# A ring of 24 gathered rows in place of four buffers of six, in a two-layer graph attention kernel

## The chip, the cores and the metric

The kernel runs on one core of one Trainium2 chip. The metric is device time in microseconds. Three runs of the kernel before took 1912.78, 1916.56 and 1921.1 us, so their median is 1916.56 us. The profiled execution took 1914.35 us, of which 1912.5 us is the span from its first to its last instruction.

## The reference

Two graph attention layers over 8192 nodes with 256 features. The adjacency is an 8192x8192 matrix that is nearly empty: an edge is drawn with chance 0.000488281, then made symmetric, with ones on the diagonal.

```
# layer 0
h  = relu(layernorm(x));  Wh = h @ W
e  = (Wh @ a[:256])[:, None] + (Wh @ a[256:])[None, :]
x  = x + leaky_relu(softmax(where(adj == 0, -1e9, e)) @ Wh, 0.2)
# layer 1
h  = relu(layernorm(x))
e  = leaky_relu(h @ a[:256] + (h @ a[256:]).T, 0.01)
x  = x + softmax(where(adj > 0, e, -9e15)) @ h
```

## The kernel before

Rows are held 128 to a tile, 64 tiles in all. Layer 0 runs on TensorE over the whole adjacency (the first 1070 us or so of the span) and is not touched by the change. While it runs, the kernel also packs the adjacency into bits and makes, for the last 44 tiles of rows, a list of each row's neighbours, sorted by their number.

Layer 1 divides the rows. The first 20 tiles are done densely on TensorE: 5 groups of 4 tiles, each group 16 chunks, each chunk 64 pairs of a weight load and a matmul of 257 columns (line 1639). The other 44 tiles are done sparsely, beside it. For each sparse tile m there are `slots[m]` neighbours to a row (24 for the first tile, then 16, 14, 14, 13, 13, 12, ... 4; 420 in all), and for each of these 420 slots, called rows here and numbered 0 to 419:

- GpSimd issues one indirect DMA that gathers 128 rows of `h_d`, one to a partition, into the tile `gat` (line 1264).
- ScalarE makes two exponentials for a batch of gathered rows (line 1321, `weights`), once the batch has landed.
- VectorE takes their larger (line 1515, `larger`), then multiplies and adds the row into `sacc` (lines 1531 and 1534, `add_row`), which raises `row_added`. When a tile has all its rows, VectorE joins, divides and adds x (`join`, `divide`, `add_x1`, the last at the fifth row of the next tile), which raises `so_ready`, and GpSimd scatters the result to `out` (line 1255, `scatter`), `OUT_LAG` = 5 batches behind.

A batch is up to 6 rows of one tile; there are 88. The tile `gat` is four buffers of six rows. GpSimd waits before the first gather of batch k until the whole of batch k-4 has been added (lines 1261 and 1262).

The dense work of a chunk is written into the same instruction streams. ScalarE makes the signs of the next chunk (line 1300, four instructions), which wait for `unit_used`, raised by TensorE every half chunk; in group 0 it also makes the high halves of V (line 1289, eight). VectorE unpacks mask bits every second chunk (lines 1456 and 1459), makes the two masks (lines 1473 and 1478), in group 0 the low halves of V (line 1438, eight), and between these adds the rows that the table `rows_by` gives to the chunk: none in chunks 0 to 2, 5 in chunk 3, about 7 in each further chunk of group 0, and 5 or 6 in each later chunk. ScalarE runs ahead of VectorE by `LEAD` = 3 rows: a chunk's batches, through the one that holds the third row after the chunk, are weighed before the next chunk's signs. Nothing is reordered by a scheduler: each engine runs its own stream in the order of the code, and each waits at its head.

Of the kernel before, what the change touches and what calls it, by code (L numbers as in the profile page):

```python
# [30 lines left out]
def two_layer_graph_attention(nc, x, adj, w0, a0, a1, key_pos, ident, tri, caps, row_ids, out):  # L31
# [30 lines left out]
    P = 128  # L62
# [71 lines left out]
    with outer:  # L134
# [13 lines left out]
        with ctx:  # L148
            def sb(name, shape, dt):
                return ctx.enter_context(nc.sbuf_tensor(name, shape, dt))  # L150
# [881 lines left out]
        RB = 4  # L1032
        BIG = 2.0 ** 100
        BS = 6
        NBUF = 4
        LEAD = 3
        FIRST = 1.35
        HEAD = 3.0
# [5 lines left out]
        for m in range(NS):  # L1044
            parts = -(-slots[m] // BS)
            for i in range(parts):
                batch.append((m, slots[m] * i // parts, slots[m] * (i + 1) // parts))
        row = [(m, s, k) for k, (m, s0, s1) in enumerate(batch) for s in range(s0, s1)]
        begin = [row.index((m, s0, k)) for k, (m, s0, s1) in enumerate(batch)]
        at = [sum(slots[:m]) for m in range(NS + 1)]  # L1050
# [5 lines left out]

        def lead_of(q):

            return sum(1 for b in begin if b < q + LEAD) if q < len(row) else len(batch)

        def ended(q):

# [9 lines left out]
        with ctx:  # L1072
# [24 lines left out]
            sS = early[:, 9 * T:9 * T + 2 * NS].rearrange("p (s t) -> p s t", s=2)  # L1097
            tS = early[:, 11 * T:11 * T + NS]
            exc = early[:, 12 * T:12 * T + NS]
            gat = sb("gat", [P, NBUF, BS, ROW], f32)  # L1100
            sacc = sb("sacc", [P, 2, 2, DV], f32)
            sout = sb("sout", [P, NOUT, D], f32)
            e8 = sb("e8", [P, 2, 2, BS], f32)
# [47 lines left out]
            masks_seen = sem("masks_seen")  # L1151
            pos_taken = sem("pos_taken")
            evn_ready = sem("evn_ready")
            den2_ready = sem("den2_ready")
            den_ready = sem("den_ready")
            rd_ready = sem("rd_ready")
            fac_ready = sem("fac_ready")
            o_ready = sem("o_ready")
            o_out = sem("o_out")
# [88 lines left out]
            @block.gpsimd  # L1248
            def _(pool):
                pool.wait_ge(mx_ready, 1)  # L1250
                nc.gpsimd.partition_all_reduce(red[:, :], red_in[:, :], P, RMAX).then_inc(M_all, 1)

                def scatter(m):
                    pool.wait_ge(so_ready, m + 1)
                    pool.indirect_dma_start(  # L1255
                        out, bass.IndirectOffsetOnAxis(ap=rec[:, m, OWN:OWN + 1], axis=0),
                        sout[:, m % NOUT, :], None).then_inc(so_out[m % NOUT], 16)

                done = 0
                for k, (m, s0, s1) in enumerate(batch):  # L1260
                    if k >= NBUF:
                        pool.wait_ge(row_added, begin[k - NBUF + 1])
                    for s in range(s0, s1):
                        pool.indirect_dma_start(  # L1264
                            gat[:, k % NBUF, s - s0, :], None, h_d,
                            bass.IndirectOffsetOnAxis(ap=rec[:, m, s:s + 1], axis=0))\
                            .then_inc(gat_in[k % NBUF], 16)
                    while done < NS and last[done] + OUT_LAG <= k:
                        scatter(done)
                        done += 1  # L1270
                for m in range(done, NS):
                    scatter(m)

            @block.scalar
            def _(act):
# [37 lines left out]
                def weights(k):  # L1313


                    m, s0, s1 = batch[k]
                    act.wait_ge(gat_in[k % NBUF], 16 * fills[k])
                    if k >= 2:
                        act.wait_ge(w8_ready, k - 1)
                    for i, scale in ((0, 1.0), (1, SLOPE1)):  # L1320
                        nc.scalar.activation(e8[:, k % 2, i, 0:s1 - s0], gat[:, k % NBUF, 0:s1 - s0, DV],  # L1321
                                             ACT.Exp, scale=scale, bias=hb[:, i, m:m + 1]).then_inc(e8_ready, 1)

                def load_rows(m):
# [59 lines left out]
            def _(dve):  # L1384
# [95 lines left out]
                def take_sums(g):  # L1480
                    dve.wait_ge(unit_used, (g * NC + NC) * 2)
                    nc.vector.tensor_tensor(den2[:, :, :], ab[:, :, bass.ds(g * G, G)],
                                            banks[:, :, D].rearrange("p (g s) -> p s g", s=2), ALU.mult)\
                        .then_inc(den2_ready, 1)
                    dve.wait_ge(den2_ready, g + 1)
                    nc.vector.tensor_tensor(den[:, :], den2[:, 0, :], den2[:, 1, :], ALU.add)\
                        .then_inc(den_ready, 1)
                    dve.wait_ge(den_ready, g + 1)
                    nc.vector.reciprocal(rd[:, :], den[:, :]).then_inc(rd_ready, 1)
                    dve.wait_ge(rd_ready, g + 1)  # L1490
                    for s in range(2):
                        nc.vector.tensor_tensor(fac[:, s, :], ab[:, s, bass.ds(g * G, G)], rd[:, :],
                                                ALU.mult).then_inc(fac_ready, 1)
# [24 lines left out]
                def add_row(q):  # L1518


                    m, s, k = row[q]
                    i = s - batch[k][1]
                    acc = sacc[:, m % 2, s % 2, :]
                    if i == 0:
                        dve.wait_ge(w8_ready, k + 1)
                    x = gat[:, k % NBUF, i, 0:DV]
                    w = w8[:, k % 2, i:i + 1]
                    if s < 2:
                        if m >= 2 and s == 0:
                            dve.wait_ge(so_ready, m - 1)  # L1530
                        nc.vector.tensor_scalar(acc, x, w, None, ALU.mult).then_inc(row_added, 1)  # L1531
                    else:
                        dve.wait_ge(row_added, q - 1)
                        nc.vector.scalar_tensor_tensor(acc, x, w, acc, ALU.mult, ALU.add)\  # L1534
                            .then_inc(row_added, 1)
# [150 lines left out]
```

## Time and profile before

| | |
|---|---|
| median of 3 runs | 1916.56 us |
| profiled execution: its time, its span | 1914.35 us, 1912.5 us |
| TensorE, VectorE, ScalarE, GpSimd busy | 88%, 63%, 51%, 34% of the span |
| L1639, the dense matmuls of layer 1 | 5120 |
| L1264, the gathers | 420, 1109 ns each in the mean |
| L1255, the scatters | 44, 1058 ns each in the mean |
| chain that ended last | PE 28%, issue 8%, POOL 4%, DVE 2% of the span |

PE is TensorE, DVE VectorE, ACT ScalarE and POOL GpSimd. A busy share is of the whole span, and layer 1 is its last 45%. "Issue" is time in which an engine waited for nothing that the profile shows. "Remote" names a releaser that the profile could not find. The ends of matmuls are modelled, so TensorE's progress is better read from the number of matmuls in a stretch than from its busy time.

### The profile page before, as it was taken

To read this page: it belongs to the slowest core of one execution; us is meant where nothing else is said; L and a number is where in the kernel's file an instruction comes from. 1 tells how busy PE (TensorE), PEld (TensorE's weight loads), DVE (VectorE), ACT (ScalarE), POOL (GpSimd) and SP (SyncE) were. 2 spreads that over 40 slices of the span, in tenths; PEclk is the share of its full clock that TensorE was granted. 3 is DMA by queue.
4 is the path that set the end of the run, shared out by engine and by line. 5 is a ranking of instruction groups with operands and counts; after the bars stand their busy time and mean duration, and the time that the engine had idled before them with its cause. 6 is when DMAs were issued, how large, how long until landed. Compare 5 with 4: busy or idle time off the path is not lost. (4 is left out here: it accounts for less than half of the span.)

```text
span 1912.5 us, 37724 instructions
## 1 busy us (share of the span) xinstructions
PE 1691.5 (88%) x13955; PEld 1391.3 (73%) x13955; DVE 1203.0 (63%) x4595; ACT 973.4 (51%) x1367; POOL 651.6 (34%) x607
## 2 busy tenths in 40 slices
PE   6888999999999999999999397677888888978878
PEld 5646888888888888888888285454666667757657
DVE  7488888988888888674444377652435445435434
ACT  5987665665666556666662375432333233323322
POOL 0000000000000000026665548755656657665562
PEclk9998999999999999999999698877889889979889
DMA  8529998888988889989994534533333333433331
GB/s 287 182 76 386 342 349 325 314 311 321 354 320 326 318 310 331 355 333 378 386 379 104 130 94 134 160 80 88 101 89 83 111 89 94 117 100 99 88 92 52
DMA packets 142801, 410.60 MB, mean 215 GB/s; under 512 B 26193, under 2 KB 90066, under 8 KB 109906
## 3 DMA queue, kind: packets, MB, share of 16 engines
q1 hardware_dynamic: 108434, 329.85, 47.6%
q0 software_dynamic: 27904, 73.43, 13.9%
q10 hardware_dynamic: 6336, 5.77, 1.0%
q8 instruction: 62, 1.02, 0.2%
q14 instruction: 65, 0.53, 0.1%
HBM read 368.94 MB, written 40.03 MB: 214 GB/s over the span
## 5 line engine op out<-in xcount | busy, mean ns | idle before, releaser
L984 PE MATMUL banks<-HV,adjT 128*128 128x257 f16 x8192 | 938.8, 274 | 16.7 <-DVE adjT L658 8.8
L984 PEld LDWEIGHTS banks<-HV,adjT 128*128 128x128 fp8e4 x8192 | 792.5, 98 | 148.2 <-DVE HV L688 23.7
L1639 PE MATMUL banks<-Vp,adjp 128*128 128x257 f16 x2560 | 540.6, 292 | 115.4 <-issue 59.2
L1639 PE MATMUL banks<-Vn,adjn 128*128 128x257 f16 x2560 | 538.1, 291 | 48.9 <-issue 47.7
L1264 POOL DMA_INDIRECT gat<-h_of_layer,rec x420 | 465.8, 1109 | 275.5 <-issue 117.9
L444 ACT ACTIVATE adj_f<-adj_i 128x2048 fp8e4<-128x2048 int32 x256 | 480.1, 1898 | 6.6 <-DMA adj_i<-in_adj 6.5
L1300 ACT ACTIVATE adjn<-h1bc,nh 128x512 fp8e5<-128x512 f32 x320 | 212.1, 716 | 446.2 <-remote 272.1
L1639 PEld LDWEIGHTS banks<-Vp,adjp 128*128 128x128 fp8e4 x2560 | 261.2, 103 | 192.3 <-issue 126.5
L1639 PEld LDWEIGHTS banks<-Vn,adjn 128*128 128x128 fp8e4 x2560 | 262.2, 103 | 124.8 <-issue 76.5
L425 POOL DMA_DIRECT2D HV<-x_after_layer x44 | 25.5, 580 | 773.4 <-DVE rank L911 741.3
L1473 DVE TENSOR_TENSOR adjn<-adjp,adjn 128x1024 uint16<-128x1024 uint16 x80 | 55.4, 692 | 334.8 <-ACT adjn L1300 296.0
L1534 DVE SCALAR_TENSOR_TENSOR sacc<-gat,w,sacc 128x257 f32<-128x257 f32 x332 | 152.5, 477 | 0.0
L492 ACT ACTIVATE pk<-banks 128x512 uint16<-128x512 uint16 x64 | 37.9, 593 | 170.3 <-PE banks L969 143.9
L695 DVE RECIPROCAL rden<-banks 128x1 f32<-128x1 f32 x64 | 10.7, 168 | 145.9 <-PE banks L984 115.3
L655 DVE TENSOR_SCALAR adjT<-pk 128x512 uint16<-128x512 uint16 x448 | 94.6, 282 | 0.0
L957 PE MATMUL banks<-w_sb,hT 128*128 128x257 f32 x256 | 68.9, 392 | 15.6 <-ACT hT L456 15.3
L627 DVE SCALAR_TENSOR_TENSOR fold<-adj_f 128x1024 int32<-128x1024 int32 x64 | 77.2, 1206 | 7.4 <-ACT adj_f L444 7.4
L418 POOL DMA_INDIRECT x_after_layer_sorted<-HV,rank x44 | 66.5, 1512 | 13.4 <-issue 12.2
L525 ACT ACTIVATE hh<-x,nmr,rstd 128x256 f32<-128x256 f32 x64 | 38.4, 601 | 53.6 <-DVE nmr L727 45.8
L1515 DVE TENSOR_TENSOR w<-e 128x5 f32<-128x5 f32 (+2 forms) x88 | 13.9, 157 | 77.8 <-ACT e L1321 58.5
L519 ACT ACTIVATE std<-mv,eps 128x1 f32<-128x1 f32 x64 | 18.8, 294 | 86.0 <-DVE mv L719 83.9
L1255 POOL DMA_INDIRECT out<-sout,rec x44 | 46.5, 1058 | 43.1 <-DVE sout L1550 31.8
(158 smaller groups left out, 1395.2 us busy)
## 6 DMA issues: line engine op xcount, KB each, us to landing
adj_i<-in_adj SPq DMA_DIRECT2D x256, 1024.0 KB
h_of_layer<-hh SPq DMA_DIRECT2D x64, 129.0 KB
hs<-h_of_layer SPq DMA_DIRECT2D x64, 129.0 KB
xt<-in_x SPq DMA_DIRECT2D x64, 128.0 KB
packed_adj<-pk SPq DMA_DIRECT2D x64, 128.0 KB
x_after_layer<-x SPq DMA_DIRECT2D x64, 128.0 KB
HV<-in_x SPq DMA_DIRECT2D x14, 512.0 KB, 8.8
gat<-h_of_layer,rec POOLq DMA_INDIRECT x420
```

The source lines that it names most:

```text
L418: pool.indirect_dma_start(x1s_d, bass.IndirectOffsetOnAxis(ap=rank[:, m:m + 1], axis=0), HV[:, T + m % SH, 0:D], None).then_inc(xs_out[m % ...
L444: nc.scalar.activation(adj_f[:, b, q * QC:(q + 1) * QC], adj_i[:, q, :], ACT.Copy, scale=2.0, saturate=False).then_inc(conv_done, 1)
L627: nc.vector.scalar_tensor_tensor(four, whole[:, 0:4 * GW], 1, whole[:, 4 * GW:8 * GW], ALU.logical_shift_right, ALU.bitwise_or)\
L655: last = nc.vector.tensor_scalar(adjT[:, b, i, :], pk[:, pb, :], PAIR << i, 6 - i, ALU.bitwise_and, ALU.logical_shift_left)
L957: last = nc.tensor.matmul(wps[t % 3][:, 0:DV], hT[:, t % 2, c, :], w_sb[:, c, :], start=(c == 0), stop=(c == 1))
L984: last = nc.tensor.matmul(acc[b][:, 0:DV], adjT_h[:, b, i, q, :, h], V0[:, jb, s, 0:DV], start=(jb == 0 and s == 0), stop=(jb == T - 1 and ...
L1255: pool.indirect_dma_start(out, bass.IndirectOffsetOnAxis(ap=rec[:, m, OWN:OWN + 1], axis=0), sout[:, m % NOUT, :], None).then_inc(so_out[m ...
L1264: pool.indirect_dma_start(gat[:, k % NBUF, s - s0, :], None, h_d, bass.IndirectOffsetOnAxis(ap=rec[:, m, s:s + 1], axis=0))\
L1300: i = nc.scalar.activation(adjn_b[:, c % 2, jb // 2, :, jb % 2], h1bc[:, g2, :], ACT.Relu, scale=-BIG, bias=nh2[:, tiles[j]:tiles[j] + 1], ...
L1473: nc.vector.tensor_tensor(part, both, part, ALU.bitwise_and).then_inc(neg_ready, 1)
L1534: nc.vector.scalar_tensor_tensor(acc, x, w, acc, ALU.mult, ALU.add)\
L1639: mm = nc.tensor.matmul(bank[2 * i + part][:, 0:DV], m[:, i * P:(i + 1) * P], V[:, j, s, 0:DV], start=(j == 0 and s == 0), stop=(j == T - ...
```

## The change

`gat` becomes a ring of 24 rows: row q lies at place q modulo 24, and the gather of row q waits until row q - 24 has been added. A batch that would run over the end of the ring is cut there, so there are 101 batches in place of 88. Six semaphores in place of four tell of landed batches, so the first gather of batch k also waits for batch k-6 to have been added. The table by which ScalarE runs ahead (`lead_of`) counts a batch only once the batch before it has begun to be added. Three semaphores of `take_sums` become one that counts to 3 in each group.

```diff
-        NBUF = 4
+        RING = 24
+        NBUF = 6
...
-                batch.append((m, slots[m] * i // parts, slots[m] * (i + 1) // parts))
+                s0, s1 = slots[m] * i // parts, slots[m] * (i + 1) // parts
+                q = sum(slots[:m])
+                wrap = -(-(q + s0 + 1) // RING) * RING - q
+                batch.extend([(m, s0, s1)] if wrap >= s1 else [(m, s0, wrap), (m, wrap, s1)])
...
-            return sum(1 for b in begin if b < q + LEAD) if q < len(row) else len(batch)
+            return sum(1 for k, b in enumerate(begin)
+                       if b < q + LEAD and (k == 0 or begin[k - 1] < q)) if q < len(row) else len(batch)
...
-            gat = sb("gat", [P, NBUF, BS, ROW], f32)
+            gat = sb("gat", [P, RING, ROW], f32)
...
-            den2_ready = sem("den2_ready")
-            den_ready = sem("den_ready")
-            rd_ready = sem("rd_ready")
+            den_steps = sem("den_steps")
...
                 for k, (m, s0, s1) in enumerate(batch):
-                    if k >= NBUF:
-                        pool.wait_ge(row_added, begin[k - NBUF + 1])
                     for s in range(s0, s1):
+                        q = at[m] + s
+                        free = max(q - RING + 1, begin[k - NBUF + 1] if k >= NBUF and s == s0 else 0)
+                        if free > 0:
+                            pool.wait_ge(row_added, free)
                         pool.indirect_dma_start(
-                            gat[:, k % NBUF, s - s0, :], None, h_d,
+                            gat[:, q % RING, :], None, h_d,
...
-                        nc.scalar.activation(e8[:, k % 2, i, 0:s1 - s0], gat[:, k % NBUF, 0:s1 - s0, DV],
+                        nc.scalar.activation(e8[:, k % 2, i, 0:s1 - s0], gat[:, begin[k] % RING:begin[k] % RING + s1 - s0, DV],
...
-                    x = gat[:, k % NBUF, i, 0:DV]
+                    x = gat[:, q % RING, 0:DV]
```

On GpSimd the start of the gathers before stands so, from the first one on: 24 gathers with no wait, then batches of 4 to 6 whose first gather waits, and scatters between them (`out<-sout`).

```order
148 L1264 DMA gat<-h_of_layer1,rec 128x258 x24
149 L1264 DMA gat<-h_of_layer1,rec 128x258 [waits row_added]
150 L1264 DMA gat<-h_of_layer1,rec 128x258 x4
151 L1264 DMA gat<-h_of_layer1,rec 128x258 [waits row_added]
152 L1264 DMA gat<-h_of_layer1,rec 128x258 x4
153 L1264 DMA gat<-h_of_layer1,rec 128x258 [waits row_added]
154 L1264 DMA gat<-h_of_layer1,rec 128x258 x5
155 L1264 DMA gat<-h_of_layer1,rec 128x258 [waits row_added]
156 L1264 DMA gat<-h_of_layer1,rec 128x258 x3
157 L1264 DMA gat<-h_of_layer1,rec 128x258 [waits row_added]
158 L1264 DMA gat<-h_of_layer1,rec 128x258 x4
159 L1255 DMA out<-sout,rec 8192x256 [waits so_ready]
```

The same start on GpSimd after the change: every gather from the 25th on carries a wait of its own, and the scatters stand between runs of 10 to 24 gathers.

```order
148 L1269 DMA gat<-h_of_layer1,rec 128x258 x24
149 L1269 DMA gat<-h_of_layer1,rec 128x258 [waits row_added] x24
150 L1258 DMA out<-sout,rec 8192x256 [waits so_ready]
151 L1269 DMA gat<-h_of_layer1,rec 128x258 [waits row_added] x10
152 L1258 DMA out<-sout,rec 8192x256 [waits so_ready]
153 L1269 DMA gat<-h_of_layer1,rec 128x258 [waits row_added] x18
154 L1258 DMA out<-sout,rec 8192x256 [waits so_ready]
155 L1269 DMA gat<-h_of_layer1,rec 128x258 [waits row_added] x13
156 L1258 DMA out<-sout,rec 8192x256 [waits so_ready]
157 L1269 DMA gat<-h_of_layer1,rec 128x258 [waits row_added] x11
158 L1258 DMA out<-sout,rec 8192x256 [waits so_ready]
```

The first scatter stood behind 49 gathers and now stands behind 48; the second behind 63 and now 58; the fifth behind 106 and now 100. No number of gathers or scatters changes.

On ScalarE, in group 0 ahead of a chunk's signs (`adjn`), a piece of before with the exponentials of two batches:

```order
480 L1321 ACTIVATE e8<-gat,hb 128x5 [waits w8_ready,gat_in0]
481 L1321 ACTIVATE e8<-gat,hb 128x5
482 L1321 ACTIVATE e8<-gat,hb 128x5 [waits w8_ready,gat_in1]
483 L1321 ACTIVATE e8<-gat,hb 128x5
484 L1300 ACTIVATE adjn<-h1bc,nh2 128x512 [waits unit_used]
```

The same place on ScalarE after the change, where the ring's end cuts a batch of five into four and one:

```order
480 L1326 ACTIVATE e8<-gat,hb 128x4 [waits w8_ready,gat_in2]
481 L1326 ACTIVATE e8<-gat,hb 128x4
482 L1326 ACTIVATE e8<-gat,hb 128x1 [waits w8_ready,gat_in3]
483 L1326 ACTIVATE e8<-gat,hb 128x1
484 L1305 ACTIVATE adjn<-h1bc,nh2 128x512 [waits unit_used]
```

The second batch of before moves one chunk on there. ScalarE has 1318 rows in place of 1292 (two for each of the 13 further batches), VectorE one more `larger` for each of them.

## Rows read from the trace of the kernel before

**Rows 1.** The page: busy time of the span; granted clock in 40 slices.

```profile
PE 1691.5 (88%) x13955; PEld 1391.3 (73%) x13955; DVE 1203.0 (63%) x4595; ACT 973.4 (51%) x1367; POOL 651.6 (34%) x607
PEclk9998999999999999999999698877889889979889
```

**Rows 2.** Stretches of layer 1: window, length, busy and (count) by engine, clock, DMA.

```profile
1121.00:1148.00 27.00, 26.89 (x242) 23.05 (x239) 23.27 (x62) 22.23 (x52) 22.56 (x13) 1.00 0.43 119
1148.00:1227.00 79.00, 60.37 (x449) 47.68 (x448) 54.82 (x148) 39.08 (x93) 64.00 (x50) 0.85 0.49 135
1235.00:1252.00 17.00, 4.29 (x13) 1.18 (x12) 1.80 (x6) 0.00 (x0) 11.17 (x12) 0.50 0.62 179
1288.00:1318.00 30.00, 15.22 (x59) 5.62 (x57) 4.83 (x15) 3.06 (x6) 21.53 (x21) 0.59 0.37 97
1330.00:1865.00 535.00, 453.54 (x3481) 351.54 (x3480) 238.16 (x699) 172.10 (x352) 333.18 (x312) 0.88 0.35 98
1865.00:1904.00 39.00, 38.87 (x341) 33.30 (x339) 18.27 (x53) 10.75 (x21) 9.73 (x10) 0.97 0.16 49
```

**Rows 3.** Timeline, POOL: start, length, line, [idle before, releaser].

```profile
1121.54 1.15 POOL L1264 DMA_INDIRECT gat<-h_of_layer,rec  x1 [22.88 <-DVE sacc L1534]
...
1134.82 2.17 POOL L1264 DMA_INDIRECT gat<-h_of_layer,rec  x1 [0.30 <-issue]
...
1248.57 0.95 POOL L1264 DMA_INDIRECT gat<-h_of_layer,rec  x1 [0.30 <-issue]
1263.38 1.01 POOL L1264 DMA_INDIRECT gat<-h_of_layer,rec  x1 [13.87 <-DVE sacc L1534]
```

**Rows 4.** Timeline, DVE: the first eight rows added.

```profile
1110.61 0.35 DVE L1531 TENSOR_SCALAR sacc<-gat,w 128x257 f32<-128x257 f32 x1
...
1119.19 0.88 DVE L1534 SCALAR_TENSOR_TENSOR sacc<-gat,w,sacc 128x257 f32<-128x257 f32 x2
...
1120.79 0.48 DVE L1534 SCALAR_TENSOR_TENSOR sacc<-gat,w,sacc 128x257 f32<-128x257 f32 x1
...
1121.79 0.87 DVE L1534 SCALAR_TENSOR_TENSOR sacc<-gat,w,sacc 128x257 f32<-128x257 f32 x2
```

**Rows 5.** Waits of ACT, 1140 to 1235 (us in total, times, longest); the first of them.

```profile
ACT e L1321 <- DMA gat<-h_of_layer,rec: 36.2, 7, 10.9
...
1157.85 0.50 ACT L1321 ACTIVATE e<-gat,hb 128x6 f32<-128x6 f32 x2 [10.92 <-DMA gat<-h_of_layer,rec]
```

**Rows 6.** Timeline, PE: two matmuls near the ends of 1235 to 1252.

```profile
1236.52 0.37 PE L1639 MATMUL banks<-Vn,adjn 128*128 128x257 f16 x1 [1.43 <-issue]
...
1252.65 0.40 PE L1639 MATMUL banks<-Vn,adjn 128*128 128x257 f16 x1 [0.33 <-issue]
```

**Rows 7.** Stretches: early and late in two runs of gathers (columns of Rows 2).

```profile
1403.00:1412.00 9.00, 9.00 (x81) 7.49 (x79) 4.69 (x14) 2.75 (x6) 7.16 (x7) 1.00 0.41 112
1412.00:1420.00 8.00, 4.30 (x29) 2.53 (x27) 0.00 (x0) 1.41 (x3) 5.06 (x6) 1.00 0.43 115
...
1670.30:1683.80 13.50, 13.50 (x123) 11.62 (x122) 7.33 (x23) 5.58 (x12) 10.76 (x10) 1.00 0.35 96
1683.80:1695.80 12.00, 6.64 (x26) 2.47 (x24) 4.54 (x15) 0.67 (x3) 8.52 (x9) 0.60 0.39 109
```

**Rows 8.** POOL, 1330 to 1865: groups of instructions, then its waits.

```profile
L1264 POOL DMA_INDIRECT gat<-h_of_layer,rec x281 | 299.9, 1067 | 194.0 <-issue 77.0 <-DVE sacc L1534 75.2 <-DVE sacc L1531 41.8
...
POOL gat L1264 <- DVE sacc L1534: 75.2, 21, 7.6
POOL gat L1264 <- DVE sacc L1531: 41.8, 10, 14.7
POOL out L1255 <- DVE sout L1550: 10.7, 3, 6.4
```

**Rows 9.** Timeline: an unpack on DVE; the gather under it and the next on POOL.

```profile
1408.74 0.69 DVE L1456 TENSOR_SCALAR adjp<-pkg 128x512 uint16<-128x512 uint16 x3
...
1408.08 1.67 POOL L1264 DMA_INDIRECT gat<-h_of_layer,rec  x1 [0.30 <-issue]
...
1412.63 0.95 POOL L1264 DMA_INDIRECT gat<-h_of_layer,rec  x1 [0.30 <-issue]
```

**Rows 10.** The page: the exponentials and the larger; all of them are layer 1's.

```profile
L1515 DVE TENSOR_TENSOR w<-e 128x5 f32<-128x5 f32 (+2 forms) x88 | 13.9, 157 | 77.8 <-ACT e L1321 58.5
...
L1321 ACT ACTIVATE e<-gat,hb 128x5 f32<-128x5 f32 (+3 forms) x176 | 41.6, 288 | 37.9 <-DMA gat<-h_of_layer,rec 37.9
```

More of the change, by code:

```diff
@@ L1483, in take_sums @@
                                             banks[:, :, D].rearrange("p (g s) -> p s g", s=2), ALU.mult)\
-                        .then_inc(den2_ready, 1)
-                    dve.wait_ge(den2_ready, g + 1)
+                        .then_inc(den_steps, 1)
+                    dve.wait_ge(den_steps, g * 3 + 1)
                     nc.vector.tensor_tensor(den[:, :], den2[:, 0, :], den2[:, 1, :], ALU.add)\
[L1487 to L1490, printed above, removed]
+                        .then_inc(den_steps, 1)
+                    dve.wait_ge(den_steps, g * 3 + 2)
+                    nc.vector.reciprocal(rd[:, :], den[:, :]).then_inc(den_steps, 1)
+                    dve.wait_ge(den_steps, g * 3 + 3)
                     for s in range(2):
```

## The prediction

> **What bounds the kernel now.** I began with the page [rows 1]. TensorE is busy for 88% of the span and GpSimd for 34%, and the clock's digits are 9 nearly throughout layer 0 and 6 to 9 in layer 1. So layer 1 is where TensorE is not fed evenly, and it is the only part that the change touches.
>
> Next I cut layer 1 into stretches [rows 2] and counted matmuls. At full clock TensorE does a matmul every 0.111 us (242 in 27.00 us), a chunk of 64 in 7.1 us. From 1148 to 1227 it did 449 in 79 us, where 0.111 each would be 50 us. From 1330 to 1865, groups 1 to 4, it did 3481 in 535 us, where 0.111 each would be 386: 149 us are lost there. From 1235 to 1252 it did 13 and from 1288 to 1318 it did 59: together 47 us for 8 us of work.
>
> The timelines then tell two different causes. In group 0 GpSimd bounds. It stood idle 22.88 us before gather 24, until the sixth row was added, and from 1121.54 to 1249.52 it then waited for nothing [rows 3]. ScalarE stood idle 36.2 us for gathers between 1140 and 1235 [rows 5], and since the signs of the next chunk come behind the exponentials on ScalarE, the masks on VectorE and the matmuls wait too.
>
> In the later groups ScalarE hardly waits for gathers, and TensorE stands idle "on issue", with its masks ready. These stretches all lie late in an unbroken run of gathers. In the run that begins at 1403, TensorE did 81 matmuls in the first 9 us and 29 in the next 8; in the run that begins at 1670, 123 in 13.5 us and then 26 in 12 [rows 7]. In the run that ends at 1249.52 it did single matmuls 0.3 to 1.4 us apart until 1252.65 [rows 3, 6]. So a long run of gathers starves TensorE, VectorE then stops adding rows because TensorE holds the masks, GpSimd runs out of released rows, and its pause ends the stretch. Each such stretch costs 8 - 29 x 0.111 = 5 us, or 12 - 26 x 0.111 = 9 us, and the clock falls to half in the longer ones (0.60 in the last row). I do not know what the shared thing is; the rows show only the coincidence.
>
> **The change part by part.**
>
> *First wait of GpSimd.* Gather 24 waited for six rows, now for one. Row 0 ends at 1110.96, row 5 at 1121.27, and the gather came 0.27 us behind the latter [rows 3, 4]. So gather 24 starts at 1111.2, 10.3 us earlier. Gathers 25 to 30 each wait for one further row: rows 3 and 4 end at 1120.07, row 5 at 1121.27 and rows 6 and 7 by 1122.7 [rows 4]. At 1.25 us from one to the next (0.95 and 0.30 [rows 3]) gather 30 starts at about 1124 to 1126, where it was at 1134.82 [rows 3]. That is 9 to 11 us, and from there GpSimd waits for nothing again, as before. I take 9.5 us; the ends are 0, if the lead is eaten (rival C), and 12.3 (gather 30 at 1122.5, 0.27 us behind row 6).
>
> *Does the lead last to the end of group 0?* ScalarE's 36.2 us of waiting for gathers cover it [rows 5], so chunks 7 to 14 move up by what the gathers move up. Behind them comes the starved stretch from 1235 to 1252, which ends with the run of gathers. Before, the run ended before gather 100, which waits for 85 rows (batch freed as a whole). Now gather 100 by itself would wait for 77, but the fifth scatter stands in front of it and waits for tile 4's result, which is made with row 85, so for 86 rows. The run ends at the same gather and therefore 9.5 us earlier. The next run ended before gather 135, which waited for 118 rows; now gathers to 134 need 111 or fewer, and 135 needs 112. The same end again, and a shorter wait behind it. Group 0: -9.5 us.
>
> *The deeper ring in groups 1 to 4.* Before, the first gather of a batch has 14 rows on average between it and the row it waits for. Now a gather has 23, but a scatter has 15 (over the 40 that stand among the gathers, 9 to 22), because the batches are smaller (420/101 = 4.2 rows) and the scatter still stands five batches behind. In 37 of 39 cases the scatter needs 4 or 5 rows more than the gather behind it. GpSimd runs in order, so the ring's depth is given back at every scatter, each 9.5 rows or two chunks: behind it the scatter and 5 or 6 gathers are free at once, and the next ones follow row by row. Before, 312 DMAs came with 34 waits for VectorE [rows 2, 8], one for 9 DMAs. I expect about the same. The bounds: if the unbroken runs fell below the length at which TensorE is starved, up to 149 us would come back; if each of the 31 scatters of that stretch [rows 8] began a run that ends in a starved stretch of 5 to 9 us, these would cost 155 to 279 us in place of the 149. Both are far out; I take +2 us, for the few gathers by which a run can now be longer.
>
> *More, smaller batches.* 13 more batches are 26 exponentials of 288 ns, 7.5 us of ScalarE, and 13 `larger` of 157 ns, 2.0 us of VectorE [rows 10]. ScalarE is busy 172 us of 535 and VectorE 238 [rows 2], and both wait for TensorE there, so this costs nothing; without that cover it would be 9.5 us. In group 0, where ScalarE is on the path, one batch is cut by chunk 10: 0.6 us, taken as 0.5.
>
> *Waits on every gather, one semaphore for three.* A wait that is already met shows no time: gathers stand 0.30 us apart with or without one. `take_sums` keeps its three waits. Nothing for either.
>
> *Gathers under VectorE's work.* With single releases more gathers start just behind a row, among VectorE's instructions. The gather at 1408.08 ran 1.67 us, across the unpack of 1408.74, where the usual one takes 0.95 [rows 9]: 0.72 more. There are 32 unpacks in groups 1 to 4, so at most 23 us of GpSimd, partly there already, and GpSimd has 128 us of waits to cover it [rows 8]. Nothing.
>
> The Trainium skill ("SBUF — State Buffer", section "SBUF: two separate sides") says that a VectorE instruction that holds both ports keeps GpSimd from writing descriptors until it is done; the 1.67 us agree. It speaks against this change, which puts gathers there: with the whole 23 us on the path the sum would be 1910 + 23 = 1933 us, and with the row's cover it stays. The same page of the skill ("Who interferes with whom") says that a DMA never contends with a compute engine. By that rule groups 1 to 4 could neither gain nor lose, and the sum would be 1916.56 - 9.5 + 0.5 = 1907.6 us; the 81 against 29 matmuls [rows 7] speak against the rule.
>
> The sum: -9.5 + 2 + 0.5 = -7 us on the profiled execution, 1914.35 to 1907.3. The median of the runs lies 2.2 us above that execution, so the prediction is 1916.56 - 7 = 1909.5, rounded to 1910 us.
>
> **The rivals.** A difference under 0.5%, 9.6 us, cannot be told from none here.
>
> *A: shorter runs feed TensorE.* Releases of single rows break GpSimd's work into pieces of 5 or 6, with a pause in each chunk. The 312 DMAs in 3481/64 = 54.4 chunks are 5.7 to a chunk, which need 5.7 x 1.37 = 7.9 us (1067 ns and 0.30 [rows 8]) against the 9.8 us that a chunk took (535/54.4). The pauses are there, if they spread. For it: nothing starves in the first 9 to 13 us of a run. Against: the scatter's wait. A third of the 149 us back is 50; with group 0 that is 57, and I take 10 off for starved stretches that grow where others go: -47, 1870 us.
>
> *B: the scatter clumps the runs.* Each scatter now waits beyond its neighbours, and behind it the run starts with 6 or 7 DMAs at once and is carried on by the rows that come. It decides if the run then reaches past 9 to 13 us, the point seen in rows 7. Priced at one more starved stretch in each of the four groups, 4 x 7 = 28, less group 0's 7: +21, 1938 us. For it: GpSimd works 7.9 of 9.8 us, so a run needs little to close up. Against: a long run also earns a long pause.
>
> *C: group 0's lead is eaten.* The starved stretch at 1235 begins after a given time of unbroken gathers and lasts until the ring is full; if more rows are fetched before GpSimd stops, the 9.5 us go into it. Then 1916 us.
>
> **How the numbers follow.** The forecast has 0.42, with its own range 1900 to 1918; a third of that lies over 0.5% faster. A has 0.22, all faster. B has 0.24, all slower. C has 0.12, no change. Faster: 0.14 + 0.22 = 0.36. Same: 0.28 + 0.12 = 0.40. Slower: 0.24. For 8 in 10 the range takes in A's price and most of B's: 1875 to 1936 us.
>
> **What would show it.** In the changed kernel's timeline gather 24 should start near 1111 with 12 to 13 us of idle time before it, not 22.88; gather 30 near 1125; ScalarE's waits for gathers in group 0 near 27 us, not 36; the first long pause of GpSimd still before gather 100, near 1240. Among the waits GpSimd's for `sout` should take most of the place of those for `sacc`. The stretch of 3481 matmuls should again take 525 to 545 us. Wrong would be: no unbroken run ending at gather 100, or that stretch outside these bounds, which decides between A and B.

## The result and the profile after

| | before | after |
|---|---|---|
| median | 1917.00 us (5 runs, 1912.78 to 1928.01) | 1957.48 us (5 runs, 1952.25 to 1970.68) |
| ratio, 95% interval | | 1.0214 (1.0163 to 1.0264) |
| profiled execution, span | 1914.35, 1912.5 us | 1964.28, 1962.2 us |

The changed kernel is slower by 40 us, outside the range; the interval lies clear of 1, and whether the loss is over 2% it leaves open. Medians, here and below, are over all runs of a kernel, and the ratios leave out the runs that fell in the chip's slower state. The page after, against [rows 1]:

```profile
PE 1693.9 (86%) x13955; PEld 1389.4 (71%) x13955; DVE 1206.7 (61%) x4608; ACT 978.9 (50%) x1393; POOL 643.9 (33%) x607
PEclk9998999999999999999998798778798798888789
```

The busy times are those of before to within 1.2%, so it is not added work that costs; the clock's digits are lower in layer 1. To find the place I compared equal work: the 3481 matmuls that took 535 us before [rows 2] are here those from 1317.1 to 1910.2. The columns are those of Rows 2.

```profile
1121.80:1248.00 126.20, 99.75 (x790) 80.47 (x788) 96.36 (x264) 77.06 (x181) 104.23 (x73) 0.89 0.50 139
1264.00:1293.00 29.00, 10.28 (x34) 3.07 (x33) 4.97 (x16) 1.83 (x4) 19.61 (x20) 0.57 0.34 92
1317.10:1910.20 593.10, 461.39 (x3482) 350.25 (x3480) 239.95 (x706) 176.01 (x373) 326.01 (x310) 0.85 0.31 88
1510.20:1521.50 11.30, 11.30 (x103) 9.81 (x101) 7.24 (x23) 4.23 (x10) 9.09 (x8) 0.99 0.36 94
1521.50:1540.80 19.30, 6.41 (x30) 2.79 (x28) 0.00 (x0) 0.55 (x1) 12.37 (x13) 0.66 0.36 96
```

The stretch begins 12.9 us earlier than before (1317.1 against 1330.0), takes 58.0 us longer (593.1 against 535.1), and what follows takes 4.6 us longer: 49.7 us, the difference of the spans. The last two rows answer to [rows 7]: a full rate of 103 matmuls in 11.3 us, then 30 in 19.3. VectorE has not one instruction in those 19.3 us, while GpSimd goes on for 13 DMAs.

What GpSimd waited for in this stretch, against [rows 8] (us in total, times, longest), and last what TensorE waited for on "issue":

```profile
POOL out L1258 <- DVE sout L1555: 161.9, 22, 14.7
...
POOL gat L1269 <- DVE sacc L1539: 21.3, 21, 9.3
POOL gat L1269 <- DVE sacc L1536: 4.3, 7, 2.3
...
PE banks L1644 <- issue: 114.4, 150, 2.5
```

TensorE's idle time on issue was 68.9 us in 117 times in the same 3481 matmuls before. Waits for `sout`, the scatter's, were 10.7 us in 3 times and are 161.9 in 22; those for rows went from 117 us to 26. Group 0's start, GpSimd's timeline, against [rows 3]:

```profile
1113.21 0.94 POOL L1269 DMA_INDIRECT gat<-h_of_layer,rec  x1 [13.30 <-DVE sacc L1536]
1117.18 0.94 POOL L1269 DMA_INDIRECT gat<-h_of_layer,rec  x1 [3.02 <-DVE sacc L1536]
...
1126.68 2.89 POOL L1269 DMA_INDIRECT gat<-h_of_layer,rec  x1 [0.30 <-issue]
...
1288.45 0.95 POOL L1269 DMA_INDIRECT gat<-h_of_layer,rec  x1 [0.30 <-issue]
1295.91 0.95 POOL L1269 DMA_INDIRECT gat<-h_of_layer,rec  x1 [6.51 <-DVE sacc L1539]
```

Gather 24 came at 1113.21 behind 13.30 us of idle time, gather 30 at 1126.68. But GpSimd then waited for nothing until 1289.4, and so passed gather 100 without a stop.

How a starved TensorE looks (timeline of PE, 1524 to 1529):

```profile
1524.18 0.27 PE L1644 MATMUL banks<-Vp,adjp 128*128 128x257 f16 x1 [0.91 <-issue]
...
1526.30 0.27 PE L1644 MATMUL banks<-Vp,adjp 128*128 128x257 f16 x1 [1.52 <-issue]
...
1528.43 0.37 PE L1644 MATMUL banks<-Vp,adjp 128*128 128x257 f16 x1 [1.53 <-issue]
```

Its masks are ready and no instruction waits for a semaphore here: a few matmuls are issued, then none for 1 to 1.5 us.

**Counting the stretches.** I listed every starved stretch of over 5 us within the 3481 matmuls: gaps of over 0.3 us between the starts of two matmuls, joined where less than 3 us lie between them. There are two executions of each kernel (the second is from the runs below). Another rule of joining moves the counts by one or two.

| means of the stretches | before | after |
|---|---|---|
| stretches | 14, 16 | 15, 16 |
| DMAs in the unbroken run ahead of one, its time | 9.5, 8.4; 12.7, 11.4 us | 7.7, 7.5; 10.3, 9.9 us |
| DMAs issued within one | 5.6, 5.9 | 8.9, 7.4 |
| length | 9.3, 9.7 us | 13.9, 12.0 us |
| GpSimd's idle time behind it | 5.5, 6.0 us | 9.1, 7.6 us |
| that pause stands before a scatter | 1, 1 | 13, 13 |

There are hardly more stretches than before, and they begin one or two DMAs earlier in a run. They are longer, with more DMAs issued within one, and the pause behind each is longer and now stands before a scatter, which needs more rows than the gather behind it.

### The profile page after: what moved, and what is told of

It is laid out like the page before. It is cut to its first block and busy times, and to the rows that moved or that the text cites. A ratio compares the mean times of both kernels' runs of the same rounds, so it can differ in the third digit from the quotient of the medians.

```text
span 1962.2 us, 37800 instructions
## 1 busy us (share of the span) xinstructions
PE 1693.9 (86%) x13955; PEld 1389.4 (71%) x13955; DVE 1206.7 (61%) x4608; ACT 978.9 (50%) x1393; POOL 643.9 (33%) x607
## 5 line engine op out<-in xcount | busy, mean ns | idle before, releaser
L1269 POOL DMA_INDIRECT gat<-h_of_layer,rec x420 | 460.8, 1097 | 168.8 <-issue 113.5
L1258 POOL DMA_INDIRECT out<-sout,rec x44 | 52.5, 1193 | 197.0 <-DVE sout L1555 191.4
L1520 DVE TENSOR_TENSOR w<-e 128x5 f32<-128x5 f32 (+5 forms) x101 | 16.3, 161 | 106.8 <-ACT e L1326 88.5
L1326 ACT ACTIVATE e<-gat,hb 128x5 f32<-128x5 f32 (+5 forms) x202 | 46.9, 287 | 50.7 <-DMA gat<-h_of_layer,rec 50.7
```

Of the source, the lines that this page charges most:

```text
L1258: pool.indirect_dma_start(out, bass.IndirectOffsetOnAxis(ap=rec[:, m, OWN:OWN + 1], axis=0), sout[:, m % NOUT, :], None).then_inc(so_out[m ...
L1269: pool.indirect_dma_start(gat[:, q % RING, :], None, h_d, bass.IndirectOffsetOnAxis(ap=rec[:, m, s:s + 1], axis=0))\
L1326: nc.scalar.activation(e8[:, k % 2, i, 0:s1 - s0], gat[:, begin[k] % RING:begin[k] % RING + s1 - s0, DV], ACT.Exp, scale=scale, bias=hb[:, ...
```

## The experiments

Two theories stood at first. Theory 1: the scatter waits for row results 15 rows behind GpSimd, while a gather may run 23 ahead; GpSimd stops at a scatter, then races, and TensorE starves. Theory 2: the deeper ring lengthens the runs by itself.

The runs divide by chip, which I had not expected. On the chip of some jobs the kernel before takes 1925 to 1931 us; on the chips of the others it takes 1752 to 1753 us. I call them the starving chip and the others. The record of the first pair names no chip; the 1917 us of the kernel before and its starved stretches are those of the starving chip. A ratio is against the kernel before on the same chip. "The stretch" is the time of the 3481 matmuls in the profiled execution.

### A later scatter (e1_lag7), on the starving chip

```
-        OUT_LAG = 5
+        OUT_LAG = 7
```

> The changed kernel with its scatters 7 batches behind in place of 5, so that a scatter hardly ever waits beyond the gather behind it. Theory 1 (the scatter's wait gathers GpSimd's releases into long unbroken runs of gathers, and TensorE is starved at the end of each): GpSimd's 171 us of waits for sout move to waits for single rows, runs get shorter, TensorE's waits on issue fall, time back to about 1900 to 1915 us. Theory 2 (the deeper ring itself makes the runs long): the runs stay at 18 to 27 DMAs, time stays at 1945 to 1965 us.

Measured 1904.77 us, ratio 0.9897 (0.9858 to 0.9936); the stretch 531.3 us.

```profile
1316.50:1847.80 531.30, 445.29 (x3480) 346.21 (x3480) 242.07 (x711) 176.10 (x372) 330.82 (x310) 0.90 0.35 98
...
POOL gat L1269 <- DVE sacc L1539: 95.6, 50, 7.5
...
POOL out L1258 <- DVE sout L1555: 7.7, 2, 5.2
```

The scatter now stands 23 rows behind, beside the gathers. Its waits are gone, the waits for rows are short ones (95.6 us in 50, and 20.0 in 12 more), and the loss of 58 us is gone with them. Group 0's gain stays (the stretch begins at 1316.5). For theory 1.

### A shallower ring (e2_depth18), on the starving chip

```
-                        free = max(q - RING + 1, ...
+                        free = max(q - 18 + 1, ...
```

> The changed kernel, but a gather waits for the row 18 back; ring, batches and scatters as changed. Theory 1 (scatter's wait): the scatter still waits for 2 to 3 rows' more than the gather behind it and stays the one wait that counts (15 rows of lead), so the time stays near 1950. Theory 2 (depth): fewer rows are free behind a pause, runs get shorter, time near 1915 to 1925 us.

Measured 1912.83 us, ratio 0.9943 (0.9885 to 1.0002); the stretch 548.8 us, the waits for `sout` 76.0 us in 13. The 1950 that I had written for theory 1 is a miss: the scatter's wait does its harm only with the depth. What counts is the distance between the two limits. In rows between a DMA and the row that it waits for, the changed kernel has up to 23 for a gather (22 in the mean, since the first gather of a batch also waits for batch k-6) and 15 in the mean for a scatter, 7 to 8 apart; here it is 17 and 15, 2 apart, and with lag 7 up to 23 and 23.

### The kernel before with an earlier scatter (e3_before_lag4), on the starving chip

```
-        OUT_LAG = 5
+        OUT_LAG = 4
```

> The kernel before with its scatters 4 batches behind in place of 5, so that a scatter needs about as many rows as the gather behind it, a lead of 14 rows in place of 18. Theory 1 (scatter's wait): somewhat slower than before, 1920 to 1940 us, with waits for sout in place of waits for sacc. Theory 2 (depth): no change, 1910 to 1922 us.

Measured 1932.3 us, ratio 1.0003 (0.9953 to 1.0052), though the median falls into the 1920 to 1940 us that I had written for theory 1; the stretch 562.5 us, within 4 us of the 558.8 that the kernel before took in its second profile. Waits for `sout` were 77.8 us in 14, in the place of waits for rows. No effect was measured. It moves the scatter's limit from 18 rows to 14, where the first gather of a batch stands too, with the last one at 18 to 19: GpSimd swings by 5 rows with or without it. So waiting for `sout` alone, 77.8 us of it, cost nothing here that can be told.

### Single releases taken out (e8, e12 and e16)

```
                         if free > 0:
-                            pool.wait_ge(row_added, free)
+                        if s == s0:
+                            free = max(free, at[m] + s1 - RING)
+                            if free > 0:
+                                pool.wait_ge(row_added, free)
```

> The changed kernel, where only the first gather of a batch waits, for the row that the batch's last gather needs: the ring of 24 with the coarse release of the kernel before. If the release of single rows (gathers that start one by one and close up to long runs) makes the loss: 1915 to 1935 us. If the scatter's wait makes it, this changes little: 1945 to 1965 us, since the scatter still waits for 4 to 5 rows more than the gathers behind it.

> The kernel of e8_whole_batch again, for a chip on which the kernel before takes 1917 to 1931 us and TensorE starves: ring of 24, only the first gather of a batch waits, for the row that its last gather needs; OUT_LAG 5. If the scatter's wait makes the change's loss: 1940 to 1965 us. If the single releases make it: 1910 to 1930 us. On a chip without starved stretches 1749 again.

> The kernel of e8_whole_batch once more, for a chip on which the kernel before takes 1917 to 1931 us: ring of 24, only the first gather of a batch waits, for the row that its last gather needs; OUT_LAG 5. If the scatter's wait makes the change's loss: 1940 to 1965 us. If the single releases make it: 1910 to 1930 us. On a chip without starved stretches 1750 again.

The first two fell on other chips: 1749.36 us, 0.9971 (0.9951 to 0.9991), and 1751.55 us, 0.999 (0.9969 to 1.0011). The third ran on the starving chip: 1962.47 us, 1.0169 (1.0119 to 1.0219), the stretch 582.2 us.

```profile
POOL out L1258 <- DVE sout L1557: 139.8, 21, 12.5
...
POOL gat L1271 <- DVE sacc L1541: 32.8, 12, 14.1
```

Without single releases the loss is there, so they don't make it. What is left of the change is the ring's depth with an unmoved scatter, and e1_lag7 and e2_depth18 take away one or the other.

### Gathers tied to TensorE's progress (e4_paced, e5_paced_lag5, e6_before_paced)

```
+                        if q >= rows_by[18]:
+                            n = max(c for c in range(C) if rows_by[c] <= q)
+                            done_at = n - 4 + (q - rows_by[n]) / (rows_by[n + 1] - rows_by[n])
+                            pool.wait_ge(unit_used, int(2 * done_at))
```

In the first with `OUT_LAG` 7, in the second with 5, in the third in the kernel before.

> As the changed kernel with scatters 7 batches behind, and from chunk 18 on each gather also waits until TensorE has done the half chunk that lies 4 chunks before the gather's place in its own chunk, so that GpSimd stops within a few gathers when TensorE is starved. If unbroken runs of gathers starve TensorE, the runs stay short (under 10 DMAs), TensorE's waits on issue fall by more than half in groups 1 to 4 and the time is 1830 to 1890 us. If the starved stretches have another cause, they stay and the time is that of the kernel without this wait, or longer because the gathers come later.

> The changed kernel with OUT_LAG 5 as it is, and from chunk 18 on each gather also waits until TensorE is no more than about four chunks behind the row it brings. Theory 1 (what costs time is an unbroken run of gathers over some 10 us, whatever starts it; the scatter's wait only makes such runs): with the runs cut, the scatter's wait does no harm, and the time comes to 1840 to 1865 us, near the 1843 of the same pacing with OUT_LAG 7. Theory 2 (the scatter's wait costs time by itself, since VectorE's rows come late behind it): the pacing brings only half of it, 1880 to 1910 us.

> The kernel before with the same wait on each gather: four buffers of six rows, released whole, OUT_LAG 5. Theory 1: the ring has no part in the gain of the pacing beyond group 0, so this comes to 1845 to 1880 us. Theory 2 (single releases are needed for the pacing to help): over 1895 us.

The first, on the starving chip, took 1842.91 us, ratio 0.9561 (0.9528 to 0.9594), the stretch 484.6 us: it beats both kernels. TensorE's idle time on issue is 38.1 us, where it was 114.4. The others fell on another chip: 1750.04 us, 0.9977 (0.9962 to 0.9993), and 1753.52 us, 1.0002 (0.9985 to 1.002). Their expectations were for a chip that starves, and stay open. What they show is that the waits cost nothing where TensorE keeps up.

### Both single changes (e7_depth18_lag7), on another chip

> The changed kernel with both single changes that each made it faster: a gather waits for the row 18 back, and OUT_LAG 7. If the deeper ring lengthens runs by itself, the two gains add in part: 1880 to 1900 us. If both only took away one thing, the scatter's long wait ahead of a ready ring, the second brings nothing: 1900 to 1915 us.

Measured 1760.33 us, ratio 1.0042 (1.002 to 1.0065), where the kernel before takes 1753.45. Whether the two gains add on the starving chip was not measured.

### Both kernels again (e9_after_again, e10_before_again), on the starving chip

> The changed kernel as it is, on another chip than its first run. One job so far (lag 7, depth 18, lag 4, paced) ran on a chip on which the kernel before takes 1925 us, the next (paced with lag 5, before paced, depth 18 with lag 7, whole batches) on a chip on which it takes 1753 us and TensorE is starved nowhere. Theory 1 (the change loses only by starved stretches of TensorE behind long runs of gathers): where the kernel before takes about 1753 us, the changed one is 1 to 8 us faster (group 0's earlier start, the rest bound by GpSimd and TensorE): 1745 to 1752; where it takes 1920, the changed one takes 1950 to 1970 again. Theory 2 (the scatter's wait costs by itself): slower than before by over 1% on every chip.

> The kernel before itself, for its profile on this chip. Where it takes about 1753 us: no starved stretch of TensorE, one unbroken run of gathers from about 1130 to the end, GpSimd without waits for VectorE in groups 1 to 4. Where it takes 1920: as in its first profile.

After 1964.31 us, ratio 1.0142 (1.0077 to 1.0207), the stretch 585.5 us; before, as a kernel of its own, 1934.32 us, 1.0018 (0.9973 to 1.0063), the stretch 558.8. In this pair the change costs 26.7 us in the stretch and gains 4.6 ahead of it, less than in the first pair: two executions of the kernel before differ by 24 us in the stretch.

### Breaks of 1 us (e11_pads, e13, e17, e14, e15)

```
                             .then_inc(gat_in[k % NBUF], 16)
+                        if q >= rows_by[18] and q % 4 == 3:
+                            for i in range(3):
+                                if pads:
+                                    pool.wait_ge(pad_set, pads)
+                                nc.gpsimd.memset(pad[:, :], 0.0).then_inc(pad_set, 1)
+                                pads += 1
```

> The changed kernel with three memsets of some 300 ns on GpSimd behind each fourth gather from chunk 18 on (about 1.0 us more per 4 gathers, no DMA among them). If a starved TensorE comes from DMAs issued without a break, breaks of 1 us in each 5 us end it on a chip that starves: 1860 to 1910 us against 1957. If it comes from GpSimd being busy, or from the number of gathers that are out, whatever their spacing: 1940 us or more. On a chip without starved stretches GpSimd, with 5.7 DMAs of 1.37 us to a chunk, is close to the bound: 88 breaks of 1 us, up to 88 us longer, 1760 to 1840.

> The kernel before with the same breaks (three memsets behind each fourth gather from chunk 18 on). Once no run is long, the ring's depth and the scatter's wait should not matter, and the changed kernel keeps its lead of group 0 alone (9 to 17 us): before with breaks 1850 to 1860 us against 1841 of the changed kernel with breaks. If the ring of single rows is what makes the breaks work: over 1870.

> The kernel of e13_before_pads, for a chip on which the kernel before takes 1917 to 1931 us. Once no run is long, the ring's depth and the scatter's wait should not matter, and the changed kernel keeps its lead of group 0 alone (9 to 17 us): before with breaks 1850 to 1860 us against 1841 of the changed kernel with breaks. If the ring of single rows is what makes the breaks work: over 1870. On a chip without starved stretches 1828 again.

> The changed kernel with the same sum of breaks, but six memsets behind each eighth gather (runs of 8 to 9 DMAs, some 11 us, breaks of 2 us). Starved stretches began 8 to 13 us into a run, so if the length of the unbroken run decides: some come back, 1850 to 1885 us. If only the mean rate of the DMAs decides: 1841 as with breaks of half the length twice as often.

> The changed kernel with two memsets (0.7 us) behind each fourth gather and OUT_LAG 7: if a break of 0.7 us is enough to end a run, GpSimd, which has 5.7 x 1.37 = 7.8 us of DMAs and then 1.0 us of breaks to a chunk, lets TensorE go on at 8.8 us a chunk and the time comes to 1825 to 1845 us. If the break has to be longer: 1860 or more.

On the starving chip the changed kernel with breaks took 1841.16 us, ratio 0.9513 (0.945 to 0.9576), below the 1860 to 1910 us that I had expected if breaks help, and though GpSimd has 210 memsets more to do in the stretch. Its timeline and the stretch:

```profile
1400.64 0.95 POOL L1272 DMA_INDIRECT gat<-h_of_layer,rec  x1 [0.30 <-issue]
1401.59 1.07 POOL L1280 MEMSET pad<- 128x257 f32 x3
1402.82 0.95 POOL L1272 DMA_INDIRECT gat<-h_of_layer,rec  x1 [0.15 <-issue]
...
1300.10:1789.70 489.60, 410.65 (x3481) 344.06 (x3479) 247.16 (x701) 174.00 (x370) 398.36 (x517) 0.94 0.38 105
```

Nothing was left out and no wait of the kernel was moved, and the stretch fell from 593.1 and 585.5 to 489.6 us. TensorE's idle time on issue fell from 114.4 us in 150 times to 14.7 in 11:

```profile
PE banks L1653 <- issue: 14.7, 11, 6.9
```

So DMAs issued one close behind the other starve TensorE, and 1 us without one behind each fourth gather ends nearly all of it. GpSimd was busier than without the breaks (81% of the stretch against 55%), so it is not its being busy. Two things changed at once, though: the run is broken, and the DMAs now come at 0.63 a microsecond (307 in 489.6 us), where in an unbroken run they come at up to 0.80 (one in 1.25 us). Which of the two counts isn't told by this run. It is not the rate over the whole stretch, which rose from 0.52 (310 in 593.1 us).

The kernel before with the same breaks took 1843.94 us on that chip, 0.9559 (0.9514 to 0.9605), the stretch 487.7 with 30.0 us idle on issue. The intervals of the two ratios overlap, so the loss of the change is gone, and the 1850 to 1860 us that I had expected are a miss. In the two profiles the 3481 matmuls begin at 1300.1 us in the changed kernel and at 1308.0 in the kernel before, so of group 0's gain 8 us can be seen, but not in the medians.

On another chip the breaks only cost: 1828.51 us in the kernel before (1.044, the stretch 490.1); in the changed kernel, six memsets behind each eighth gather 1831.24 us (1.0438, 499.0), and two behind each fourth with `OUT_LAG` 7 1795.17 us (1.0243, 463.3). With breaks, a starving chip and another take the same 490 us. What length of run, or of break, or what rate is enough was not settled, since the last two did not run on the starving chip; their expectations stay open.

### The changed kernel on a chip that does not starve (e18_after_third)

> The changed kernel as it is. If the scatter's wait costs only through starved stretches of TensorE, then on a chip on which the kernel before takes about 1753 us the changed one takes 1745 to 1758 us, no difference that can be told. If the wait costs by itself: over 1765 us. On a chip on which the kernel before takes 1920 to 1930 us it takes 1950 to 1970 for the third time, and this stays open.

Measured 1749.56 us against 1752.37, ratio 0.9977 (0.9963 to 0.9991). The stretch, and GpSimd's waits in it:

```profile
1275.60:1703.50 427.90, 398.64 (x3482) 341.37 (x3480) 241.89 (x700) 175.16 (x368) 332.54 (x314) 0.97 0.44 123
...
POOL gat L1269 <- DVE sacc L1539: 16.1, 53, 0.3
...
POOL out L1258 <- DVE sout L1555: 0.3, 1, 0.3
```

314 DMAs without a pause of over 0.3 us, and TensorE has no wait on issue: 427.9 us for what took 593.1. One wait for `sout` is left, of 0.3 us. That it was long only where VectorE had been held up by a starved TensorE is how I read it. Here GpSimd is the bound (332.5 us of DMAs and 0.30 between two), neither the ring nor the scatter is met, and the change is worth 0.2% (0.1 to 0.4%), against the 1.4 to 2.1% that it costs on the starving chip. That fits the first theory of its expectation, no difference of note, and not the second, over 1765 us.

Put in one order, the profiles of the starving chip show what the stretch follows, the distance between the two limits and not the wait for `sout` alone. The third column is counted from the program: the gathers that are free at once, in the mean, when a scatter's wait has ended. The last one is TensorE's idle time on issue in the stretch.

| kernel | rows between: gather, scatter | free behind a scatter | waits for `sout` | stretch | TensorE on issue |
|---|---|---|---|---|---|
| e1_lag7 | up to 23, 23 | 0.2 | 7.7 us | 531 us | 71 us |
| before, two executions | 14 to 19 by batches, 18 | 0 | 10.7, 7.3 | 535, 559 | 69, 88 |
| e2_depth18 | 17, 15 | 3.1 | 76.0 | 549 | 73 |
| e3_before_lag4 | 14 to 19 by batches, 14 | 3.8 | 77.8 | 563 | 89 |
| e16_whole_batch_third | 18 to 22 by batches, 15 | 6.0 | 139.8 | 582 | 104 |
| after, two executions | up to 23, 15 | 7.1 | 161.9, 160.7 | 593, 586 | 114, 97 |

With differences of 24 us between two executions, the order within the upper four rows proves nothing; that of the last two kernels against the others holds in three executions of three.

The starved stretches themselves go the same way, counted by the rule of the first table. With the scatter moved (e1_lag7) there are 15 again, of 9.9 us and 5.9 DMAs in the mean, with 5.0 us of idle time behind, once before a scatter: the lengths of the kernel before, with the ring as deep as in the changed one. With whole batches and an unmoved scatter (e16_whole_batch_third) there are 15 of 12.9 us and 8.1 DMAs, with 7.7 us behind, 11 times before a scatter: the changed kernel's.

## Why the prediction was wrong

**First wait of GpSimd: right.** Gather 24 was forecast near 1111 with 12 to 13 us of idle time, and layer 0 had ended 1.7 us later in this execution: it came at 1113.21 behind 13.30. Gather 30 was forecast at 1125 and came at 1126.68, 8.1 us ahead of [rows 3], 9.9 from the same end of layer 0.

**Group 0, -9.5 us: right in sign, its end told wrongly.** ScalarE's waits for gathers from 1140 to 1235 fell from 36.2 us [rows 5] to 22.5 (27 forecast). The run did not end before gather 100: VectorE, fed earlier, had added row 86 at 1246.1, ahead of the fifth scatter at 1254.0. The starved stretch of 1235 to 1252 [rows 2] moved to 1264 to 1293, where 34 matmuls took 29 us. What was gained at the start of the 3481 matmuls was 12.9 us in the first pair and 4.6 in the second. Rival C did not happen.

**The deeper ring in groups 1 to 4, +2 us: the step that failed.** The stretch of 3481 matmuls was forecast at 525 to 545 us and took 593.1. The term measured +58.0 us in the first pair and +26.7 in the second. The facts in it were right: the scatter stands 15 rows back, 4 to 5 rows beyond the gather right behind it, and its waits took the place of the others. One count was low: that gather is held by the wait for batch k-6, and those behind it are freer, so 7 gathers in the mean (2 to 12) are free at once behind a scatter, where I had written 5 or 6. The conclusion was wrong, that "the ring's depth is given back at every scatter". I treated the scatter's wait as a cap on GpSimd's lead, the same as a shallower ring. It is the lower turning point. GpSimd stops until its lead has fallen to 15 rows, and is then free to race to 22 or 23. Those 7 to 8 rows are in hand, beside those that VectorE adds meanwhile, when a stretch begins: GpSimd issued 10 to 16 DMAs within 8 of the 15 stretches of the first execution and 11 to 16 within 6 of 16 of the second, and in the kernel before 10 or more within 1 of 14 and 2 of 16. The pause behind is longer as well. Both limits at one distance (e1_lag7), or nearly so (e2_depth18), take the loss away, and with the first the stretches have the length of before. That the rows in hand are the very DMAs that lengthen a stretch is argued from these counts, not measured by itself.

**Rival B: right in kind, mispriced.** It was this mechanism, priced at one more stretch in each group (+28). The number of stretches hardly grew (14 and 16, then 15 and 16); each grew by 4.6 and 2.3 us in the mean, and the pause behind it by 3.6 and 1.6. I had priced the count where the length moved. The bound that the rows gave, 155 to 279 us of starved time in place of 149, contained the result (593 - 386 = 207 us lost); I named it "far out", and the range, with its end at 1936 us, stopped short even of rival B's own 1938.

**More batches, more waits, gathers under VectorE's work: no cost, as forecast.** VectorE was busy 3.7 us more (2.0 forecast for it) and ScalarE 5.5 (7.5 forecast), and on the other chip all of it lies in a kernel that is 0.2% faster. The gathers took 1097 ns each in the mean, where they took 1109 before, so they were not held up more. The Trainium skill ("SBUF — State Buffer", section "SBUF: two separate sides") says that whichever of VectorE and GpSimd takes their shared pair of ports first has it for its whole instruction, and the other is blocked. No run here tells which instruction held up a gather such as the 2.89 us one above.

**The rule that a DMA never contends with a compute engine** ("SBUF — State Buffer", section "Who interferes with whom", in the Trainium skill): the trace of the starving chip disagrees, with 30 matmuls in 19.3 us under 13 DMAs and 489.6 against 593.1 us by breaks alone. The trace of another chip agrees, with 3482 matmuls in 427.9 us under 314. By which way the DMAs reach TensorE's progress no run shows. By the rule I would have forecast 1907.6 us, which is wrong too, for the chip of the measurement.

## What to carry to other kernels

When two kinds of work share an in-order queue and each waits on progress of its own, move both limits together: the further apart they are, the more the queue swings between standing still and racing, and a neighbour that suffers from the racing pays for the depth. A buffer is deepened only together with what stands behind it in the queue: with `OUT_LAG` 7 the deeper ring took 0.990 of the kernel before on the starving chip, and with 5 it took 1.014 to 1.021. Where a stream of small gathers has time to spare, tie it to the progress of the engine that must not starve, which with `OUT_LAG` 7 brought 4.4% on a chip that starves, and with `OUT_LAG` 5 cost nothing where none does; fixed breaks brought 4.9% there and cost 4.4% in the kernel before on another.

## What the hardware showed that I had not expected

The same program takes 1925 us on one chip and 1753 on others, steadily: the kernel before had medians of 1924.85, 1930.69 and 1926.5 us on the starving chip, and 1753.45, 1753.01 and 1752.37 on three others. Layer 0 takes the same on both: the mask of layer 1's first chunk is ready at 1081 to 1085 us in every profile. The gathers themselves take nearly the same: 0.95 us each in the median there and 0.96 to 0.97 on the others, 0.30 apart.

What TensorE shares with the stream of gathers stays open. It is not the traffic as a whole: the DMA engines are 36% busy while it starves, at 96 GB/s, and 44% at 123 GB/s where it does not. It does not look like late loading of its instructions either: one queue moved 16 KB of instructions for each 128 matmuls or so, on both kinds of chip, and nothing between 1514.1 and 1547.2 us, while the matmuls of 1521.6 to 1541.1 crawled. The number of DMAs ahead of a stretch is not fixed: 8 to 10 in the mean at 1.3 us apart, but in group 0, where 73 DMAs took 126 us, 1.7 us apart and with no wait among them, TensorE did 790 matmuls beside them. That speaks for the spacing of the DMAs and against the mere length of a run, without settling it.

One thing more differs between the chips. The page tells how long a gather takes to land (2.9 us) only for the chips that do not starve:

```profile
gat<-h_of_layer,rec POOLq DMA_INDIRECT x420
```

is the row of the changed kernel's first profile, and on the other chip (e18_after_third) it reads

```profile
gat<-h_of_layer,rec POOLq DMA_INDIRECT x420, 2.9
```

The records of landing are not complete on the chip that starves: 12,722 in this profile of the changed kernel and 13,088 in that of the kernel before, against some 20,270 on the others. Every run here, the timed ones too, was taken with records of its span and clock, so no run tells whether the starved stretches are there in an execution that nothing records. The time that was measured contains them, and the prediction was about that time.
